# Softmax attention in a four-layer kernel: maxima behind the numerators in group 0, layer-norm tiles one a unit, and the last quotient and output tiles in quarters and in two banks

## The reference, cut to what matters

```
x = x + _L0_xattn_ref(_layernorm(x), ctx_768, ...)
x = x + _L0_ffn_ref(_layernorm(x), ...)
x = x + _L1_xattn_ref(_layernorm(x), ctx_768, ...)     # this stage
x = x + _L1_ffn_ref(_layernorm(x), ...)

def _L1_xattn_ref(x, context, w_q, b_q, w_k, b_k, w_v, b_v, w_o, b_o):
    q = x @ w_q + b_q;  k = context @ w_k + b_k;  v = context @ w_v + b_v
    # 16 heads of 32 features each
    scores = jnp.einsum('bqhd,bkhd->bhqk', q, k) * scale
    weights = jax.nn.softmax(scores, axis=-1)
    out = jnp.einsum('bhqk,bkhd->bqhd', weights, v).reshape(B, Lq, D)
    return out @ w_o + b_o
```

## Time and profile before

| What | Value |
|---|---|
| median of three runs | 1825.77 us |
| the profiled execution, its own time | 1826.94 us |
| its span, first to last instruction | 1824.4 us |
| TensorE busy | 1600.0 us, 88% |
| VectorE, ScalarE, GpSimd busy | 68%, 63%, 60% |
| mean granted TensorE clock | 0.954 |
| one batch of the attention stage (the third residual of group 1 at 958.47 us and at 1055.42 us) | 96.95 us |

### The profile page before, as it was taken

One profiled execution on the slowest core, in us unless ns is written; L12 is line 12 of the kernel. 1 busy time (PEld: TensorE's weight loads), 2 busy tenths in 40 slices (PEclk: granted clock), 3 DMA queues, 4 the chain that ended last, 5 costly groups with the idle time before them and its releaser, 6 DMA issues. The chain is left out here.

```text
span 1824.4 us, 31159 instructions
## 1 busy us (share of the span) xinstructions
PE 1600.0 (88%) x8930; PEld 724.6 (40%) x8930; DVE 1248.1 (68%) x1737; ACT 1156.2 (63%) x1902; POOL 1093.5 (60%) x789
## 2 busy tenths in 40 slices
PE   5799478998999957999999999999999964999998
PEld 2355233443444423334434344434444312444443
DVE  2778687888888664868676767676767636456553
ACT  4576488888888622675656666566657535665662
POOL 3577356888989832675756666665747544455442
PEclk9899789999999977999999999999999987999999
DMA  8221000000000022111111102011201001001001
GB/s 295 95 80 57 1 1 1 1 1 1 0 1 1 1 75 81 36 53 36 36 53 29 56 25 56 27 54 31 56 25 41 23 1 69 24 23 46 23 23 47
DMA packets 60479, 72.30 MB, mean 40 GB/s; under 512 B 14417, under 2 KB 40017, under 8 KB 59857
## 3 DMA queue, kind: packets, MB, share of 16 engines
q1 hardware_dynamic: 56944, 62.22, 10.8%
q10 hardware_dynamic: 3424, 8.91, 1.3%
HBM read 37.40 MB, written 8.39 MB: 25 GB/s over the span
## 5 line engine op out<-in xcount | busy, mean ns | idle before, releaser
L1383 DVE TENSOR_REDUCE s_mx<-bank 128x1 f32<-128x512 f32 x512 | 336.7, 686 | 188.9 <-PE bank L1492 183.1
L1299 ACT ACTIVATE s_E<-bank 128x512 f32<-128x512 f32 x512 | 292.6, 595 | 200.1 <-PE bank L1506 175.3
L1223 POOL TENSOR_TENSOR s_E<-s_E 128x1024 f32<-128x1024 f32 x128 | 299.0, 2356 | 126.5 <-PE bank L1514 119.1
L962 PE MATMUL bank<-f_zh,f_w1q 128*128 128x512 f16 x512 | 200.2, 391 | 38.3 <-DVE f_y L830 35.6
L1492 PE MATMUL bank<-s_KA,s_QA 96*128 96x512 f16 x512 | 193.3, 388 | 24.3 <-DMA s_KA<-s_qkh 14.1
L620 POOL TENSOR_TENSOR f_y<-f_y,f_t 128x511 f32<-128x511 f32 x128 | 173.5, 1356 | 66.2 <-DVE f_y L830 66.2
L963 PE MATMUL bank<-f_zl,f_w1q 128*128 128x512 f16 x512 | 200.1, 391 | 0.0
L1506 PE MATMUL bank<-s_QA,s_KA 97*128 97x512 f16 x512 | 195.7, 383 | 4.5 <-ACT s_E L1299 2.8
L1216 POOL TENSOR_TENSOR s_qkl<-s_qkf,s_qkh 128x512 f16<-128x512 f32 x64 | 75.3, 1176 | 189.5 <-ACT s_qkh L1277 189.3
L1677 POOL TENSOR_TENSOR m_xl<-m_xf,m_xh 128x512 f16<-128x512 f32 x64 | 89.9, 1413 | 112.8 <-ACT m_xh L1720 112.8
L1514 PE MATMUL bank<-s_E,s_V 128*32 128x512 f32 x1024 | 136.3, 605 | 2.6 <-ACT s_E L1299 2.6
(11 more groups left out here) (234 smaller groups left out, 3860.9 us busy)
## 6 DMA issues: line engine op xcount, KB each, us to landing
X<-in_x SPq DMA_DIRECT2D x8, 1024.0 KB, 6.9
s_QA<-s_qkh SPq DMA_DIRECT2D x256, 32.0 KB, 1.8
out_x<-X SPq DMA_DIRECT2D x8, 1024.0 KB, 4.3
s_KA<-s_qkh SPq DMA_DIRECT2D x248, 32.0 KB, 1.9
a_cf<-in_ctx SPq DMA_DIRECT2D x8, 768.0 KB, 4.8
s_cf<-in_ctx SPq DMA_DIRECT2D x8, 768.0 KB, 4.8
w1raw<-in_w ACTq DMA_DIRECT2D x1, 4096.0 KB, 13.4
w2raw<-in_w ACTq DMA_DIRECT2D x1, 4096.0 KB, 29.6
```

What stands on the lines that cost most here:

```text
L962: e.matmul(hb(odd, j), w1q[:, cols], zh(odd, c), start=(c == 0), stop=False)
L1223: e.tensor_tensor(into, into, other, ALU.add).then_inc(s_sum.sem, 1)
L1299: e.activation(E[:, SLOT[k] + h, :], SC[u % 2][:, :], ACT.Exp, scale=1.0 / float(np.sqrt(DH)))\
L1383: e.tensor_reduce(mx[:, q, h:h + 1], MX[q % 2][:, :], AX.X, ALU.max).then_inc(s_red.sem, 1)
```

## The change: what it does

1. In group 0, TensorE issues the first two maxima tiles of the next group behind `attend` and `denominators` of the group before, instead of in front of them. Groups 1 and 3 keep the old order, and group 2 has them in front of its query projection as before.
2. The four normalisations of the next batch's tiles, two at unit 15 of group 0 and one each in units 0 and 1 of group 1, become one each in units 0 to 3 of group 1.
3. The fourth transposed chunk moves from unit 10 to unit 11 of group 1, and with it its `high` and `low` from unit 11 to unit 12.
4. Behind the loop, the last quotient runs in quarters: a reciprocal, its multiplication, bias, high part and low part for 128 columns at a time. An output tile waits for its own quarter alone.
5. The last four output tiles alternate between banks `R6` and `R7`.

```
-    T_UNITS, STATS_UNITS = (4, 6, 8, 10), (1, 3, 6, 10)
+    T_UNITS, STATS_UNITS = (4, 6, 8, 11), (1, 3, 6, 10)
@@ gpsimd, behind the loop
-            divided(B - 1, NG - 1)
+            for q in range(TT):
+                e.wait_ge(s_ah.sem, s_ah.count(B - 1, NG) + q)
+                cols = slice(q * P, (q + 1) * P)
+                e.tensor_tensor(atl[:, NG - 1, cols], AT[:, 1, cols], ath[:, NG - 1, cols], ALU.subtract)\
+                    .then_inc(s_al.sem, 1)
@@ scalar, behind the loop
-            divided(B - 1, NG - 1)
+            s_o.wait(e, B - 1, 0)
+            for q in range(TT):
+                cols = slice(q * P, (q + 1) * P)
+                e.wait_ge(s_an.sem, s_an.count(B - 1, NG) + q)
+                e.activation(AT[:, 1, cols], AT[:, 1, cols], ACT.Identity, bias=bv[:, NG - 1:NG]).then_inc(s_ab.sem, 1)
+                e.wait_ge(s_ab.sem, s_ab.count(B - 1, NG) + q)
+                e.activation(ath[:, NG - 1, cols], AT[:, 1, cols], ACT.Copy).then_inc(s_ah.sem, 1)
@@ vector, in step
-                        if u == UNITS - 1:
-                            normalise(e, b + 1, (0, 1))
-                    if m == 1 and not last and u < 2:
-                        normalise(e, b + 1, (u + 2,))
+                    if m == 1 and not last and u < TT:
+                        normalise(e, b + 1, (u,))
@@ vector, behind the loop
-            for i in range(4):
+            s_av.wait(e, B - 1, NG)
+            for i in range(TT):
+                cols = slice(i * P, (i + 1) * P)
                 reciprocals(B - 1, NG - 1, i)
-            divide(B - 1, NG - 1)
+                e.wait_ge(s_rc.sem, s_rc.count(B - 1, 4 * (NG - 1) + i + 1))
+                e.tensor_tensor(AT[:, 1, cols], AT[:, 1, cols], DEN[:, cols], ALU.mult).then_inc(s_an.sem, 1)
             for q in range(TT):
-                residual(B - 1, q)
+                residual(B - 1, q, (R6, R7)[q % 2])
@@ tensor, output()
                 if c == 0:
-                    if q == 0:
+                    if end:
+                        e.wait_ge(s_al.sem, s_al.count(b, NG) + q)
+                    elif q == 0:
                         s_al.wait(e, b, NG)
-                    take(6)
-                    reader[6] = (s_res, b, q + 1)
+                    take(i)
+                    reader[i] = (s_res, b, q + 1)
@@ tensor, step()
-                if m != 2 and nxt:
+                if m in (1, 3) and nxt:
                     for k in range(MAX_AHEAD):
                         maximum(*nxt, k)
                 if div:
                     attend(*div, TT - 1)
                     denominators(*div, 0)
+                if m == 0 and nxt:
+                    for k in range(MAX_AHEAD):
+                        maximum(*nxt, k)
@@ tensor, behind the loop
-                    output(B - 1, q, c)
+                    output(B - 1, q, c, 6 + q % 2, True)
```

More of the change, by code:

```diff
@@ L1392, in divide, with residual @@
                 e.tensor_tensor(AT[:, m % 2, :], AT[:, m % 2, :], DEN[:, :], ALU.mult).then_inc(s_an.sem, 1)
-            def residual(b, q):
+            def residual(b, q, bank=R6):
                 s_bo.wait(e, b, q + 1)
                 s_o.wait(e, b, q + 1)
-                e.scalar_tensor_tensor(tile(b, q), R6[:, :], 1 / WS, tile(b, q), ALU.mult, ALU.add)\
+                e.scalar_tensor_tensor(tile(b, q), bank[:, :], 1 / WS, tile(b, q), ALU.mult, ALU.add)\
                     .then_inc(s_res.sem, 1)
@@ L1530, in transposed, with output @@
                 reader[7] = (s_zl, b, c + 1)
-            def output(b, q, c):
+            def output(b, q, c, i=6, end=False):
                 if c == 0:
-                    if q == 0:
+                    if end:
+                        e.wait_ge(s_al.sem, s_al.count(b, NG) + q)
+                    elif q == 0:
                         s_al.wait(e, b, NG)
-                    take(6)
-                    reader[6] = (s_res, b, q + 1)
+                    take(i)
+                    reader[i] = (s_res, b, q + 1)
                 rows = lambda x: lambda c: x[:, c, q * P:(q + 1) * P]
                 cols = lambda x: lambda c: x["o"][:, c * D:(c + 1) * D]
-                last = product(R6[:, :], rows(ath), rows(atl), cols(wh), cols(wl), c, NG)
+                last = product(banks[i][:, :], rows(ath), rows(atl), cols(wh), cols(wl), c, NG)
                 if c == NG - 1:
```

## The result

The changed kernel takes 1813.28 us, the median of four runs (1811.41 to 1815.67), beside 1825.18 for the kernel before. The ratio is 0.9936, with a 95% interval of 0.9916 to 0.9955: faster by 0.64%, where 1813 was forecast.

The account below looks back on a forecast made before the run. TensorE, 97 of 100 us busy, was taken to bound the batch loop, paying each wait in full. Terms -2.8 - 6.7 + 3.0 + 0 - 6.5 = -13.0 us gave 1813, range 1808 to 1817.

Parts of the forecast that it names:

- Group 0: Group's start: 1.16 us DMA wait becomes reduction waits of 0.57 and 0.19; gains 2.8 us over batches 1 to 7.
- Group 1's start: Third maximum's 1.11 us wait behind the paired normalisations goes whole in batches 1 to 6: 6.7 us gained.
- The first rival: Group 1: GpSimd's subtraction delays the fourth normalisation, first transposed chunk waits 0.8 us six times: +5, 1818; chance 0.16.
- Unit 11 instead of 10: Group 1: chunk's 0.77 us wait goes, value products in unit 12 wait 1.27 for `low`: +3.0 us over six batches.
- Batch 0: Group 1 there: fourth chunk only gains, fourth normalisation may delay the first chunk; taken as 0, within 1.3 us.
- Behind the loop: After the loop: quotient in quarters starts outputs 4.2 us earlier, three 1.0 us waits go; 6.5 gained (4 to 8).
- the two readings of the clock: Output tiles: full clock returns at the same moment, 1496.3 (5.1 us gained), or 4.6 us after the restart (7.3).
- The sum: All terms together: -13.0 us on the profiled 1826.94, giving 1813.9; as a median 1813, range 1808 to 1817.
- rival 2: New waits on reductions or `low` smaller than worked out: 1800 for both, 1805 to 1808 for one; chance 0.12.
- rival 3: After the loop: only 3 to 4 us gained, from lasting low clock or costly small operations: 1816; chance 0.06.
- rival 4: Group 1: two of four normalisations run into GpSimd, 2.2 us each; slower than before, 1834; chance 0.04.
- rival 5: Change fails its purpose, for example DMA wait returns behind `denominators`, group 0 gives nothing: 1816; chance 0.06.

Follow-up runs that it names:

- The pair set against GpSimd: Changed kernel with no normalisation in unit 2 of group 1 and two in unit 3: 1820.79 us, ratio 0.9977 to the kernel before.
- the exchange of two lines: Changed kernel with the low part written before the residual on VectorE in a unit that has both: 1806.37 us, ratio 0.9901 to the kernel before.

## Why the prediction was right, point by point

**What bounds the loop.** Right. TensorE was taken to pay each of its waits in full, and the groups changed by what their waits changed: a batch went from 96.95 to 95.71 us (the same residual at 956.30 us and at 1052.01 us), where 95.9 was forecast.

**Group 0.** The mechanism was right and the places only partly. The DMA wait went, and a wait on the reductions took its place, worked out as 0.57 and 0.19 us and measured as 0.42 + 0.16 = 0.58 and 1012.61 - 1012.24 - 0.22 = 0.15. Wrong was the number of batches. The prediction counted the DMA wait in 1 to 7, but the six waits of the earlier trace rows held one of group 3 of batch 1, and batches 1 and 7 had none; they lost 0.59 and 0.43 us. This is the sixth wait, 3.8 us behind the copy of row maxima at 888.77 us, which stands in the last unit of group 2 of batch 1:

```profile
892.57 0.60 PE L1492 MATMUL bank<-s_KA,s_QA 96*128 96x512 f16 x2 [0.38 <-DMA s_KA<-s_qkh]
```

Batches 2 to 6 gained 0.56 to 0.88, 3.2 us where 2.0 were forecast for them; in all 2.2 and not 2.8. At the place of the earlier trace rows itself TensorE gained 0.42 us, as worked out, but that group became 0.57 shorter; where in the group the other 0.15 came from was not followed up. Group 1's first maxima didn't meet their DMAs in batches 2 to 6, as forecast, though the room was smaller than stated: 1028.49 + 1.9 is 1030.4 and not 1030.2. In batch 1 group 1 gained 0.26 us in this profile and 0.65 in the second one, where 0.61 was forecast.

**Group 1's start.** Right: taking the edit back costs 1.14 us in a group where 1.11 was forecast. The first rival, that the fourth normalisation runs into GpSimd, did not come about, and by just the 0.12 us that the prediction had worked out: in all six batches the normalisation began 0.11 or 0.12 us ahead. That it fell on this side is partly luck: a working over five rows could well be off by as much. The pair set against GpSimd shows what a stalled last normalisation costs, 1.1 us a batch, and not the 0.8 of the rival.

**Unit 11 instead of 10.** Right in its place, sign and size. The forecast was a wait of 1.27 us in the place of 0.77; the exchange of two lines took 1.27 us out of the group, and the chunk at unit 10 was 0.45 us better than at 11. This edit makes the kernel slower; the others cover it.

**Batch 0.** Taken as 0 within 1.3 us, it was a loss of 1.1, of which 1.00 stands in group 1 (25.87 to 26.87). The prediction's sentence that the fourth chunk only gains there was wrong. The first chunk now waits for the fourth normalisation, and the value products wait for `low` (1.34 us idle) longer than the fourth chunk did before (1.06). Taking back the normalisations returns 0.47 us of it, and taking back unit 11 returns 0.55.

```profile
PE bank L1467 <- DVE s_zl L1386: 1.3, 1, 1.3
PE bank L129 <- DVE s_z L111: 1.1, 1, 1.1
```

These are its waits from 740 to 780 us in the changed kernel.

**Behind the loop.** 7.0 us in place of 6.5. From the first reciprocal to the first output matmul it took 2.68 us against 2.79 forecast. (The sign given for it, about 4 us behind the reciprocal's end, did not fit the prediction's own sum, which puts it 1.9 us behind that end; it was 1.7.) The small operations went nearly as guessed, 0.29 us for the 128-column product against 0.69 for 512, 0.40 and 0.31 against 0.72 and 0.63, 0.43 against 1.15. The single edits give 3.7 us for the quarters and 3.2 for the two banks. Of the two readings of the clock the second was the nearer. The full clock was back 5.4 us behind the restart of TensorE, not at the old moment of 1496.3:

```profile
1488.06 0.63 PE L1469 MATMUL bank<-s_woh,s_atl 128*128 128x512 f16 x1
1488.49 0.50 PE L1467 MATMUL bank<-s_woh,s_ath 128*128 128x512 f16 x1
1488.83 0.38 PE L1468 MATMUL bank<-s_wol,s_ath 128*128 128x512 f16 x1
```

How long it stays low is not fixed: 4.6 us in the kernel before, 4.2 with the quotient whole.

**The sum.** In the two profiled executions: 1.0 us came before the stage, where the code is the same; batch 0 lost 1.1, groups 0 gave 2.2 and groups 1 of batches 1 to 6 gave 3.7, as forecast (6.7 - 3.0). The last group in front of the quotient took 1.7 us longer (the granted clock was 0.93 there before and 0.86 after, see below), and behind it 7.0 were gained; together 11.1, and the spans are 11.2 apart. So the forecast gain of 13.0 us was too large. It missed 1.1 in batch 0 and 0.6 in group 0 and had 0.5 too little behind the loop. In the medians the gain is 11.9 us, 1825.18 to 1813.28. That the time came out within 0.3 us of the forecast 1813 is luck: the runs' own scatter is 4 us, and the 1.0 us before the stage and the 1.7 us of the last group are in no term of the sum.

**The rivals.** None of the five came about. The new waits of rival 2 were there, at 0.58, 0.15 and 1.27 us; the tail gave 7.0 us and not the 3 to 4 of rival 3; no normalisation in the changed kernel's stage took more than 0.81 us, where rival 4 wanted two of 2.7; and the DMA wait of rival 5 did not come back.

## What to carry to other kernels

When an instruction is moved by one unit, read the queue of every engine that it is moved on: here a read-out landed behind an instruction that waits for TensorE's latest work, and that cost more than the wait it was to remove. Work put in front of a waiting instruction often covered another latency where it stood; place the waiting pair in the middle, so that each half has its cover. And where whole times scatter by 4 to 6 us, compare a landmark that stands once in every round of the loop: it shows 0.1 us.

## What the runs showed of the hardware that was not expected

The granted clock of the last group differs from run to run. There TensorE works with short waits, and the clock falls to its lower level, 1.2 GHz, for part of the time in some runs and not in others of one and the same kernel. The window from the last copy of row maxima to the first reciprocal, in the first and in the second profile of the changed kernel:

```profile
1455.80:1480.70 24.90, 17.66 (x89) 3.38 (x88) 6.28 (x8) 13.75 (x24) 17.44 (x10) 0.86 0.00 0
```

```profile
1453.80:1475.40 21.60, 14.36 (x89) 3.02 (x88) 6.26 (x8) 13.61 (x24) 17.43 (x9) 1.00 0.00 0
```

The same 89 matmuls take 3.3 us more at 0.86 than at 1.00 of the clock. The spans of these two profiles are 1813.2 and 1806.7 us, with the same lengths of the groups within 0.5 us. Of the 6.5 us between them 3.3 are this window; 2.1 came before the stage and the rest behind it. Over the 14 profiles of this document the same stretch takes 21.6 us in six, 23.1 to 23.3 in three (the kernel before among them) and 24.7 to 24.9 in five. That is as much as most edits here bring. It may be why whole times put the fourth chunk's edit at zero once and at 2.6 us the other time, but that is not shown: in the profiled executions the stretch was the same on both sides of each comparison, 24.92 us in the first and 21.63 in the second.
